# Two gather stages of a graph kernel: the last two node blocks worked side by side, their messages stored in pieces, two self-loop products moved into earlier visits

## The reference

```
h  = relu(layernorm(x))                                   # layer 0: attention over edges
e  = exp(q[src] . k[dst]);  he = v[src] * e / segment_sum(e, dst)
x1 = h + segment_sum(he, dst)
y  = layernorm(x1) * g + b
x  = x + x1 + gelu(y @ W_in + b_in) @ W_out + b_out       # W_in 256 x 1024
h  = relu(layernorm(x))                                   # layer 1: relations
h_all = einsum('ni,rio->nro', h, W)                       # 8 relations: 2048 numbers a node
agg   = segment_sum(h_all[src, edge_type], dst)
z  = gelu(agg + h @ loop_w + h_bias + h)
x  = x + layernorm(z) * gamma + beta
```

## Time and profile before

| | us |
|---|---|
| median of three runs | 1514.89 |
| the profiled execution's own time | 1513.77 |
| its span | 1511.9 |
| PE busy | 1178.1 (78%) |
| DVE busy | 908.2 (60%) |
| POOL busy | 896.2 (59%) |
| ACT busy | 459.8 (30%) |
| DMA, mean | 170 GB/s |

### The profile page before, as it was taken

The page is one execution under the profiler, slowest core; times in us unless marked ns, Lnnn a source line. Parts: engine busy times, 40 slices in busy tenths (PEclk is TensorE's granted clock), DMA queues, the critical chain, the costliest instruction groups (busy, mean ns, idle before and its releaser), DMA issues. The chain is left out here.

```text
span 1511.9 us, 18542 instructions
## 1 busy us (share of the span) xinstructions
PE 1178.1 (78%) x5460; PEld 854.6 (57%) x5460; DVE 908.2 (60%) x2797; ACT 459.8 (30%) x1150; POOL 896.2 (59%) x960
## 2 busy tenths in 40 slices
PE   5875779999899999899999897677666666666663
PEld 2442667777677777677777765444444444444441
DVE  5664877767777767777777774213444443444443
ACT  5553234454444453444443443200000000000000
POOL 1655767555555555555555540077777777777770
PEclk9997999999999999999999999967888888888885
DMA  6548867676666666666666641134444444444441
GB/s 211 145 129 265 261 210 238 213 233 207 213 202 206 222 223 200 211 194 191 223 209 197 214 131 67 60 115 128 127 132 130 128 129 132 133 125 131 130 131 34
DMA packets 136570, 256.31 MB, mean 170 GB/s; under 512 B 40390, under 2 KB 85424, under 8 KB 133266
## 3 DMA queue, kind: packets, MB, share of 16 engines
q0 software_dynamic: 50176, 154.19, 33.5%
q1 hardware_dynamic: 85330, 99.71, 20.7%
q10 hardware_dynamic: 960, 1.18, 0.2%
HBM read 192.76 MB, written 62.25 MB: 169 GB/s over the span
## 5 line engine op out<-in xcount | busy, mean ns | idle before, releaser
L1039 POOL DMA_INDIRECT arena<-qv_tab,srcs x392 | 397.7, 1015 | 299.5 <-PE ps L1226 214.4
L1606 POOL DMA_INDIRECT arena<-h_all,typs x392 | 377.0, 962 | 132.8 <-issue 131.3
L1669 PE MATMUL ps<-arena 128*128 128x256 f32 x784 | 280.0, 493 | 174.6 <-DMA arena<-h_all,typs 171.5
L1669 PEld LDWEIGHTS ps<-arena 128*128 128x128 f32 x784 | 169.8, 238 | 272.1 <-DMA arena<-h_all,typs 218.0
L1226 PE MATMUL ps<-arena 128*128 128x264 f32 x784 | 217.8, 401 | 73.5 <-DVE arena L1368 73.1
L1226 PEld LDWEIGHTS ps<-arena 128*128 128x128 f32 x784 | 137.8, 191 | 124.5 <-DVE arena L1368 95.0
L1429 DVE TENSOR_TENSOR arena<-arena,ps 128x512 f32<-128x512 f32 x196 | 134.3, 685 | 104.2 <-PE ps L1215 94.7
L1278 PE MATMUL ps<-wrel,arena 128*128 128x512 f32 x400 | 188.1, 596 | 1.4 <-ACT arena L1126 1.4
L1215 PE MATMUL ps<-arena 128*128 128x264 bf16 x1176 | 167.8, 280 | 18.3 <-DVE arena L1352 16.7
L1215 PEld LDWEIGHTS ps<-arena 128*128 128x128 bf16 x1176 | 144.1, 145 | 46.4 <-DVE arena L1352 17.1
L1620 ACT ACTIVATE arena<-ps 128x256 f32<-128x256 f32 x49 | 18.8, 384 | 426.7 <-PE ps L1681 407.5
(11 more groups left out here) (150 smaller groups left out, 1399.6 us busy)
## 6 DMA issues: line engine op xcount, KB each, us to landing
h_all<-arena SPq DMA_DIRECT2D x25, 1024.0 KB, 6.0
arena<-dst SPq DMA_DIRECT2D x49, 256.0 KB, 4.4
rel<-arena SPq DMA_DIRECT2D x77, 128.0 KB, 2.3
arena<-k_tab SPq DMA_DIRECT2D x49, 198.0 KB, 2.8
att<-arena SPq DMA_DIRECT2D x52, 132.0 KB, 2.8
qv_tab<-arena SPq DMA_DIRECT2D x25, 256.0 KB, 3.0
arena<-qv_tab,srcs POOLq DMA_INDIRECT x392, 4.3
arena<-h_all,typs POOLq DMA_INDIRECT x392, 2.8
```

Of the source, the lines that this page charges most:

```text
L1039: pool.indirect_dma_start(out=rowbuf[:, u * T + t, 0:2 * D], out_offset=None, in_=qv_tab, in_offset=bass.IndirectOffsetOnAxis(ap=srcs[:, v ...
L1606: pool.indirect_dma_start(out=rowbuf[:, u * T + t, :], out_offset=None, in_=h_all, in_offset=bass.IndirectOffsetOnAxis(ap=typs[:, v * T + ...
L1669: last = nc.tensor.matmul(ps[:, 6 + u, 0:D], ind[:, u, t, :], rowbuf[:, u * T + t, :], start=(t == 0), stop=(v == 0 and t == T - 1))
```

## The change

Five edits, all in the two gather stages.

1. First stage, blocks 23 and 24: `bank_x` and `bank_y` give them banks 3, 2 and 1, 0 (the key banks, free after the last scores). DVE prepares both and then normalizes both in one series of steps (`roots`, each step for both blocks ahead of its wait); PE turns both before the fourth message of block 22; `hidden` and `gelu` of block 24 work on 53 columns instead of 128. ACT's order changes with it: both `y_features` ahead of the fourth eviction of block 22, `keep_h1` later, both `relu` ahead of the messages.
2. The messages of blocks 23 and 24 are stored in four pieces of 512 numbers per row, each after its own eviction (`store_quarters`); those of block 24 have 53 rows instead of 128. The gathers name `h_all[0:N*R]` as their table.
3. Second stage: the turns and products of the self-loop of blocks 23 and 24 (`turn`, `features`, `loop_part`, `loop_sum`) go behind the carry of visits 45 and 47.
4. Second stage: `combine` is split into `loop_sum` and the rest; hz gets three buffers and z two; blocks 23 and 24 are finished together.
5. POOL adds the last `shift_result`s after all `residual`s.

```diff
+        def roots(own, blocks):
+            for var, h, t, r in blocks:
+                own.did(nc.vector.tensor_scalar(h, var, 0.5, 0.5 * EPS, ALU.mult, ALU.add))
+            own.wait()
...
             def bank_x(m):
-                return 6 if m < NBLK - 1 else 1
+                return 6 if m <= LASTM else 3 if m % 2 else 1
             def bank_y(m):
-                return 7 if m < NBLK - 1 else 0
+                return 7 if m <= LASTM else 2 if m % 2 else 0
+            def rows_of(m):
+                return P if m < NBLK - 1 else LASTP
...
+                def store_quarters(m):
+                    n = rows_of(m)
+                    for c in range(4):
+                        sp.wait_ge(msg_taken, 4 * m + c + 1)
+                        sp.dma_start(hall_v[m * P:m * P + n, c * 512:(c + 1) * 512],
+                                     msg[0:n, m % 2, c * 512:(c + 1) * 512]).then_inc(msg_out[m % 2], 16)
...
-                for m in range(LASTM - 1, NBLK):
+                for m in range(LASTM - 1, LASTM + 1):
                     store_messages(m)
+                for m in range(LASTM + 1, NBLK):
+                    store_quarters(m)
...
                 for m in range(LASTM + 1, NBLK):
                     prepare(m)
-                    normalize(m)
+                normalize(*range(LASTM + 1, NBLK))
...
+            EARLY = {G - 2 - 2 * (NBLK - 1 - m): m for m in range(LASTM + 1, NBLK)}
...
                     add_up(v)
                     carry(v)
-                    if m is not None:
-                        loop_part(m)
-                for m in range(LASTM + 1, NBLK):
-                    turn(m)
-                    loop_part(m)
+                    if v in EARLY:
+                        turn(EARLY[v])
+                    if loop_of(v) is not None:
+                        loop_part(loop_of(v))
...
                 for v in range(G):
                     m = block_of(v)
+                    if v - 1 in EARLY:
+                        loop_sum(EARLY[v - 1])
                     if m is not None:
                         copy_h1(m)
                     indicators(v)
                     if v % 2 and v > FIRST:
+                        loop_sum(block_of(v - 1))
+                        if v in EARLY:
+                            copy_h1(EARLY[v])
                         combine(block_of(v - 1))
                         finish(block_of(v - 1))
+                loop_sum(LASTM)
                 combine(LASTM)
                 finish(LASTM)
                 for m in range(LASTM + 1, NBLK):
-                    copy_h1(m)
                     combine(m)
-                    finish(m)
+                finish(*range(LASTM + 1, NBLK))
```

More of the change, by code:

```diff
@@ L680, in root @@
                 own.wait()
+        def roots(own, blocks):
+            for var, h, t, r in blocks:
+                own.did(nc.vector.tensor_scalar(h, var, 0.5, 0.5 * EPS, ALU.mult, ALU.add))
+            own.wait()
+            for var, h, t, r in blocks:
+                own.did(nc.vector.tensor_scalar(t.bitcast(I32), h.bitcast(I32), 1, None, ALU.logical_shift_right))
+            own.wait()
+            for var, h, t, r in blocks:
+                own.did(nc.vector.tensor_scalar(r.bitcast(I32), t.bitcast(I32), -1.0, float(HALF_ROOT), ALU.mult, ALU.add))
+            own.wait()
+            for _ in range(3):
+                for var, h, t, r in blocks:
+                    own.did(nc.vector.scalar_tensor_tensor(out=t, in0=r, scalar=r, in1=h, op0=ALU.mult, op1=ALU.mult))
+                own.wait()
+                for var, h, t, r in blocks:
+                    own.did(nc.vector.scalar_tensor_tensor(out=r, in0=t, scalar=1.5, in1=r, op0=ALU.subtract, op1=ALU.mult))
+                own.wait()
         def flag(eng, n):
@@ L1320, in _ @@
                 turn_h1(LASTM)
-                for c in range(4):
-                    message(LASTM, c)
+                message(LASTM, 0)
+                message(LASTM, 1)
+                message(LASTM, 2)
                 for m in range(LASTM + 1, NBLK):
                     turn_y(m)
+                message(LASTM, 3)
+                for m in range(LASTM + 1, NBLK):
                     hidden(m, 0)
@@ new lines, in combine, with finish @@
+                def combine(m):
+                    if m >= 2:
+                        dve.wait_ge(o_ready, m - 1)
+                    dve.wait_ge(rel_in[m % 2], 16 * (m // 2) + 16)
+                    nc.vector.tensor_tensor(z[:, m % 2, :], zin[:, m % 2, :], hz[:, m % 3, :], ALU.add).then_inc(z_ready, 1)
+                def finish(*blocks):
+                    for m in blocks:
+                        dve.wait_ge(g_ready, m + 1)
+                        dve.nop(nofuse=True)
+                        own.did(nc.vector.bn_stats(zst[:, m % 2, :], z[:, m % 2, :]))
@@ L1733, in finish @@
                     own.wait()
                     dve.nop(nofuse=True)
[L1735 removed]
+                    for m in blocks:
+                        own.did(nc.vector.bn_aggr(zmv[:, m % 2, :], zst[:, m % 2, :]))
                     own.wait()
[L1737 to L1738 removed]
+                    roots(own, [(zmv[:, m % 2, 1:2], vv[:, m % 2, 0:1], vv[:, m % 2, 1:2], vv[:, m % 2, 2:3]) for m in blocks])
```

123 lines of the change are left out of this document (71 added, 52 removed).

## The result

The changed kernel took **1508.66 us** (median of 11 runs, 1506.13 to 1512.33), the kernel before 1514.89 in the same job (11 runs); the ratio is 0.996, 95% interval 0.9946 to 0.9974. The forecast was 1511.5, range 1504.5 to 1517.5. The interval leaves out 1, so the gain of about 6 us (0.4%) is real; it reaches from 0.26% to 0.54%, so whether it is above the 0.3% of the forecast is open. By a bound of 2% it is no change. The profiled execution took 1506.81 us against 1513.77, its span 1505.0 against 1511.9, at a mean granted clock of 0.915 against 0.913.

The account below looks back on a forecast made before the run. POOL's indirect loads in the second gather stage held the largest share of the chain of waits, untouched by the change. Terms +7.5 + 0.7 - 11.5 = -3.3 us gave a median of 1511.5 us, range 1504.5 to 1517.5.

Parts of the forecast that it names:

- the first stage up to the last eviction: End of first gather stage: block 24's last message eviction starts at 968.9 us, 4.8 us earlier than before.
- The 2.2 us kept for the range: Block 24's hidden, first stage: up to 2.2 us more gained if only columns counted; taken as 0 in the forecast.
- The 934.2 for block 23's normalized rows: First stage, DVE: block 23 is normalized near 934.2 us; if as late as 936.1, 1.0 us would be lost.
- the stores: First stage's end: block 24's 53-row pieces go through one DMA engine and land 7.5 us later, at 985.7.
- Rival A: First stage's stores: 53-row pieces do spread over the engines, stores' term -6.3, kernel at 1497.8 us; chance 0.10.
- rival B: First stage's stores: pieces don't overlap on their engine, landing at most 994.4, kernel 1517.9 to 1520.3 us; chance 0.08.
- Visit 48: Second stage: indicators wait for block 24's self-loop sum, then PE does four pairs instead of one; +0.7 us.
- the range's 2.2 for the clock: Visit 48, second stage: allowance on the faster side of the range for PE's clock, -2.2 us.
- Rival C: Second stage, visit 48 at half clock: sums come 4.9 us late instead of 0.7, kernel at 1515.8 us; chance 0.10.
- the tail: Second stage's end: blocks 23 and 24 finished together, last result at 1495.7 instead of 1507.45, -11.75 us.
- The last store: End of kernel: two result stores follow at once, block 23's first packets ahead of the 53 on that engine; +0.25 us.
- within 0.3%: Whole kernel: time changes by no more than 0.3%, what a measurement can't tell from no change; chance 0.59.

Follow-up runs that it names:

- indicators first, with spread stores: Changed kernel with both 53-row stores spread (64 rows; 48 and 5) and, in visits 46 and 48, indicators ahead of the self-loop's sum: 1493.64 us, ratio 0.9861.
- the kernel that finishes one by one: Changed kernel, but blocks 23 and 24 are finished one behind the other at the end of the second stage: one run, 1515.4 us.
- two comparisons of medians: Changed kernel against the kernel before, in two jobs: 1508.66 us, ratio 0.996; then run again, 1510.59 us, ratio 0.9971.
- the kernel with spread stores: Changed kernel, but block 24's four pieces have 64 rows and its result is stored as 48 and 5 rows: 1495.20 us, ratio 0.9877 to before.
- the first four experiments: Changed kernel with block 24's pieces of 128 rows (0.9885), 54 rows (0.9892), one 53-row store (1624.28 us), or blocks 23 and 24 stored whole (0.9905).
- the last three runs: On one chip, before at 1514.12 us: stores spread (0.9877), that plus indicators ahead of the self-loop's sum (0.9861), and the changed kernel again (0.9971).

## Why the prediction was right, step by step

**Right: the first stage up to the last eviction.** 4.8 us earlier was predicted, 4.97 measured. The feed comes at 945.74 - 0.88 = 944.86 (said: 945.0). The 53 columns of block 24's hidden gained nothing. The groups of both, with busy time and mean ns of one:

```profile
L1297 PE MATMUL ps<-arena,win 128*128 128x128 f32 x32 | 3.7, 275 | 0.0
L1297 PE MATMUL ps<-arena,win 128*128 128x53 f32 x32 | 3.7, 273 | 0.0
```

The 63 weight loads beside the 64 matmuls took 7.11 us, 0.11 us each whether 128 or 53 columns stream. That is near the 107 ns that the Trainium skill gives for 128 columns of weights ("TensorE: Matmul & The Clock Gate", section "LDWEIGHTS (loading the stationary operand)"). The 2.2 us kept for the range weren't needed. The 934.2 for block 23's normalized rows was over a microsecond too early: the two interleaved roots delay it, and PE turned it at 936.34 - 0.88 = 935.46. It cost little, as the third message ended only shortly before: PE waited 0.22 us for DVE.

**Right in the mechanism, too large by 2.0: the stores.** Said +7.5 (bounds +6.1 to +12.2), measured +5.47. The term that was mis-sized is the stretch from block 24's first eviction to the gather, 23.9 us said and 21.97 measured (964.52 to 986.49). The four pieces took 18.4 us (first bytes at 965.8, last at 984.2), 0.087 us a packet instead of 0.095: 1.7 of it. The row of their own size had come closer, but by luck: no stretch ran at 0.088, the first 16 packets took 0.17 us each and the rest 0.080 (last section). The other 0.2 is in lead and landing. The evictions' extra 0.17 makes up the rest. Undone in two ways (54 and 128 rows) and done alone in the kernel before, the cause held each time. Rival A (the pieces spread) and rival B (they don't overlap, over 24 us of gap) are out by the gap of 16.2 us.

**Visit 48: +0.7 said, -1.13 in the first pair of traces.** The path was as predicted: product, sum, indicators, then four pairs without a gap; the indicators end 494.7 us behind the first gather, where the forecast had 1475.7 - 980.14 = 495.6. The pairs then ran partly at the low level (clock 0.50 from 1482 to 1484) and the product behind them at the high one (1.03 us, before 1.91). The price of a pair was too high at both levels, as 1.13 and 2.08 us are those of pairs that stand alone: in one run the four take 3.73 us at clock 1.00, 0.93 a pair (indicators first, with spread stores), and 6.71 at 0.50 for most of it, 1.68 a pair.

```profile
1471.24 3.73 PE L1731 MATMUL ps<-arena 128*128 128x256 f32 x16
```

By its own terms the range's 2.2 for the clock should also have been 2.0 (0.7 + 1.3). Over seven traces the mean difference is +0.7, but single ones lie between 6.07 and 8.87 us, so the agreement of that mean is luck. Rival C (all at half clock) isn't wrong as a mechanism: in the kernel that finishes one by one, the sixteen matmuls had the clock at 0.50 for most of their 6.71 us. It was a risk of each execution, and I had given it as a case that either holds or doesn't. Its price of +4.9 was too high for the reason above.

**Right: the tail.** -11.75 said, -11.77 measured. A slot a step was the right model: 12.93 us against 4.96 + 2.2 + the 5.80 from block 22's sum (1482.75) to the start behind its result (1488.55). **The last store: +0.25 said, -0.35 measured**: block 23's rows don't hold up the 53 by anything that shows. Why the end came closer than before no run separates.

The sum of -3.3 became -7.8 without the 0.88 from ahead of the change: 2.0 from the stores, 1.8 from visit 48's clock in that pair, 0.6 from the last store. In the two comparisons of medians it was -6.2 and -3.5 us, so the median of 1508.66 lies inside the range, 2.8 us under the 1511.5, and the first gain is nearly twice the forecast one. The likeliest case, "within 0.3%" with a chance of 0.59, is at the edge: the ratio is 0.4% under 1 in the first comparison and 0.3% in the second. The mechanism was right in each part; the stores' term is what was mis-sized for certain, and how much of visit 48's share is chance of one execution the traces leave open.

What the prediction didn't do is turn its own finding into the alternative: it named 53 rows on one engine as the price of the pieces and still took the stage end as given. One row more would have been the change to propose.

## What to carry to other kernels

Before splitting or shrinking a DMA, look at how many rows it has: 53 rows went through one engine, 54 through nine, and the smaller store took 12 us more than one padded to 128 rows. Pad the rows where the target has room, and split off a remainder where it hasn't (48 + 5 saved 1.8 us). When engines get earlier and the next stage doesn't, read the gap behind their last instruction and the DMA share in it; 0.06 to 0.07 for long is one engine of 16.

## What the runs showed of the hardware that I had not expected

- On one engine the packets of the four pieces were slow at first and faster later: 16 packets of 2 KB from 965.8 to 968.5, 0.17 us each, then 0.080 (12, 22 and 26 GB/s in the windows above). In six traces at this speed the faster rate begins 2.6 to 2.7 us behind the first bytes. PE and ACT falling silent isn't what brings it: in the same six, PE's last matmuls end 1.1 to 1.2 us behind its beginning (969.6 in the changed kernel), and ACT's evictions later still. The last store of the kernel before has the same shape with one store alone and no engine at work: gaps and 9 to 27 GB/s up to the 21st slice, then 24 GB/s in the mean, 0.043 us for 1 KB. So the forecast's 0.059, and the 0.117 it gave as a bound, contained a slow start. The single store of 53 rows of 8 KB ran at about 0.3 us a packet (0.08 for 2 KB) almost from its start. More pieces in the queue don't explain these two; the cause stays open.
- TensorE's granted clock in the same 5 us of the same code differed from execution to execution: sixteen matmuls took 5.41, 5.29, 6.38 and 6.71 us, and those with the indicators first 3.73 in one run of the kernel with spread stores.
- Two kernels can be compared across jobs only by ratio: the kernel before took 1514 to 1518 us (medians) in three jobs and 1626 in the one of the first four experiments, though that was the same chip as for the last three runs. There the second stage took 561 to 565 us from its first to its last gather against 494 to 497 in all other traces, and 17% to 18% of the span in the chain that ended last stand under "another core or an unknown queue". Why it was slow stays open.
